# Re-ordered start and end of an attention block: four queries and half of the modulation ahead of the first scores, low parts ahead of the last reciprocals

## The reference

```python
mod = (silu(c) @ wmod).reshape(16, 6, 1, 256)      # sa, ca, ga, sb, cb, gb
ga, gb = sign(ga) * max(|ga|, 0.25), sign(gb) * max(|gb|, 0.25)
h = layernorm(x) * (1 + ca) + sa
q, kv = h @ Wq.T, h @ Wkv_down.T                   # 8 heads of 64; latent of 64
x = x + ga * (softmax(q @ (kv @ Wk_up.T).T / 8) @ (kv @ Wv_up.T)) @ Wo.T
h = layernorm(x) * (1 + cb) + sb
x = x + gb * (h @ weight.T + pooled(h) @ disha)    # pooled: sums of h over 4 pieces of 64
```

## Time and profile before

| | us |
|---|---|
| median of 3 runs | 3176.31 (3176.28 to 3179.29) |
| the profiled execution, its own time | 3175.94 |
| its span, first to last instruction | 3174.1 |
| PE busy in the span | 3115.8 (98%) |
| POOL busy | 2556.5 (81%) |
| DVE busy | 2295.4 (72%) |
| ACT busy | 1729.6 (54%) |

### The profile page before, as it was taken

How to read it: one execution, slowest core, us unless ns; L and a number is a source line. 1 busy time by engine, 2 the same in 40 slices (tenths; PEclk the granted TensorE clock), 3 DMA queues, 4 the chain that set the end, 5 groups by cost and what they waited for, 6 DMA issues and landing times.

```text
span 3174.1 us, 44918 instructions
## 1 busy us (share of the span) xinstructions
PE 3115.8 (98%) x15394; PEld 1907.2 (60%) x15394; DVE 2295.4 (72%) x2466; ACT 1729.6 (54%) x3209; POOL 2556.5 (81%) x1521
## 2 busy tenths in 40 slices
PE   6999999999999999999999999999999999999997
PEld 5556656556665665656566565666656656565555
DVE  5667777776777777777777777767777777776764
ACT  3555555555555555555555555555555555555543
POOL 2888787888878888787887878888788887887886
PEclk8999999999999999999999999999999999999998
DMA  2111111111111111111111111111111111111111
GB/s 83 41 44 58 49 53 44 52 60 44 55 54 58 48 41 58 48 64 48 44 61 44 57 45 48 64 44 54 51 61 46 43 57 48 61 44 38 55 44 40
DMA packets 161250, 162.89 MB, mean 51 GB/s; under 512 B 58112, under 2 KB 109440, under 8 KB 161024
## 3 DMA queue, kind: packets, MB, share of 16 engines
q1 hardware_dynamic: 161024, 160.03, 15.4%
HBM read 74.40 MB, written 17.33 MB: 29 GB/s over the span
## 4 chain that ended last, share of the span: by engine, by line
PE 88%; DVE 4%; issue 3%; ACT 2%; POOL 2%; DMA 1%; SPq 0%; POOLq 0%; ACTq 0%; DVEq 0%
PE ps_mix L601 26%; PE ps_score L622 15%; PE ps_max L647 14%; PE ps_score L624 13%; PE ps_side L587 7%; PE ps_side L713 4%; PE ps_side L732 3%; PE ps_side L699 2%; POOL prob_sum L987 2%; DVE neg_max L1138 1%; ACT probs L818 1%; PE ps_side L720 1%; PE ps_side L689 1%; PE ps_side L665 1%; DVE mixed L1106 1%
## 5 line engine op out<-in xcount | busy, mean ns | idle before, releaser
L987 POOL TENSOR_TENSOR prob_sum<-prob_sum,probs 128x1024 f32<-128x1024 f32 x768 | 1890.5, 2462 | 317.1 <-ACT probs L818 242.8
L1138 DVE TENSOR_REDUCE neg_max<-ps_max 128x1 f32<-128x1024 f32 x1024 | 1238.0, 1218 | 420.6 <-PE ps_max L647 411.5
L818 ACT ACTIVATE probs<-ps_score 128x512 f32<-128x512 f32 x2048 | 1112.5, 596 | 548.5 <-PE ps_score L624 537.7
L601 PE MATMUL ps_mix<-probs,values 128*64 128x512 f32 x4096 | 935.4, 598 | 0.8 <-ACT probs L818 0.8
L622 PE MATMUL ps_score<-query,key_hi 128*128 128x512 f32 x2048 | 877.3, 428 | 9.3 <-DVE query L1176 6.1
L624 PE MATMUL ps_score<-query_m,key_lo 128*128 128x512 f32 x2048 | 806.1, 394 | 0.0
L647 PE MATMUL ps_max<-key_hi,query 128*128 128x512 f32 x2048 | 642.6, 395 | 11.9 <-DVE neg_max L1138 11.5
L601 PEld LDWEIGHTS ps_mix<-probs,values 128*64 128x64 f32 x4096 | 271.3, 136 | 531.0 <-issue 529.8
L622 PEld LDWEIGHTS ps_score<-query,key_hi 128*128 128x128 f32 x2048 | 384.1, 188 | 255.1 <-ACT probs L818 102.3
L647 PEld LDWEIGHTS ps_max<-key_hi,query 128*128 128x128 f32 x2048 | 380.9, 188 | 112.2 <-DVE neg_max L1138 20.8
L987 POOL TENSOR_TENSOR prob_sum<-probs 128x1024 f32<-128x1024 f32 x128 | 319.3, 2495 | 129.2 <-ACT probs L818 129.2
(11 more groups left out here) (200 smaller groups left out, 2833.8 us busy)
## 6 DMA issues: line engine op xcount, KB each, us to landing
query_m<-query SPq DMA_DIRECT2D x128, 512.0 KB, 3.2
recip<-recip_scratch SPq DMA_DIRECT2D x254, 128.0 KB, 2.9
x_in<-in_L_attn_x_dram SPq DMA_DIRECT2D x32, 512.0 KB, 4.6
x_mid<-in_L_attn_x_dram SPq DMA_DIRECT2D x64, 256.0 KB, 3.7
out_dram<-x_mid SPq DMA_DIRECT2D x64, 256.0 KB, 2.2
denoms<-recip SPq DMA_DIRECT2D x508, 1.0 KB, 1.7
gates<-gates_scratch SPq DMA_DIRECT2D x16, 256.0 KB, 4.3
query_m<-max_row SPq DMA_DIRECT2D x128, 4.0 KB
```

The source lines that it names most:

```text
L601: last = nc.tensor.matmul(ps_mix[j * R:j * R + R, :], values[par][:, k, :], probs[:, (STEPS * z.c + s) % RING, j * HALF:(j + 1) * HALF], s ...
L818: nc.scalar.activation(probs[:, (STEPS * z.c + s) % RING, half * HALF:(half + 1) * HALF], ps_score[half], ACT.Exp, scale=SCALE).then_inc(e ...
L987: nc.gpsimd.tensor_tensor(out=total[:, :], in0=before, in1=probs[:, now % RING, :], op=ALU.add).then_inc(adds_done, 1)
L1138: nc.vector.tensor_reduce(neg_max[:, m:m + 1], ps_max[m % 2][:, :], AX_X, ALU.max, negate=True).then_inc(maxima_done, 1)
```

## The change

Nothing of the arithmetic changes except the number of instructions in three places.

1. **Head.** PE makes only half of the modulation (16 of 32 matmuls) ahead of the first projections; the other half becomes a side piece `mod_out` on step 57. DVE writes batch 0's `mod1` itself, and POOL's copy of it is gone from the head.
2. **Head.** Only queries 0 to 3 are made in slot -1 (before: 0 to 5). Queries 4 to 7 move to steps 0, 2, 4 and 6 of slot 0 (before: 6 and 7, on steps 0 and 4). Query 0 goes ahead of the second `latent`. Two of four `wo_fold` pieces move to steps 10 and 14 of slot 0, both `weight_t` to steps 18 and 22.
3. **Head.** Statistics and `apply` for the first half of batch 1 move from step 63 of slot -1 into slot 0 (statistics on step 1, apply on step 2); those of the second half from steps 1 and 2 to steps 3 and 4.
4. **Tail.** `mixed_hi` and `mixed_lo` of chunks 0 and 1 go ahead of `divide_last` in ACT's and DVE's queues, `mixed_lo` of chunk 2 right behind it, and `out_proj` of all four chunks onto four consecutive steps ahead of the first `norm2_t`. In `divide_last` each reciprocal is followed by its multiplication. `FFN_HI` of the tail goes from step 3 to 2.
5. **Everywhere.** `w_ffn_lo` becomes two instructions of 256 columns: on steps 21 and 23 of a middle slot, both on step 2 of the tail.

```diff
-FFN_GATE, FFN_HI, FFN_LO = (1, 19), (3, 21), (3, 21)
+FFN_GATE, FFN_HI, FFN_LO = (1, 19), (2, 21), ((2, 2), (21, 23))
...
 LAST = {
-    "mixed_hi": (1, 2, 5, 6),
-    "mixed_lo": (1, 2, 5, 6),
-    "out_proj": (2, 4, 8, 10),
-    "norm2": (4, 5, 9, 11),
-    "norm2_t": (7, 9, 12, 13),
-    "h2_split": (7, 9, 12, 13),
-    "ffn": (9, 11, 14, 15),
+    "mixed_hi": (0, 0, 2, 2),
+    "mixed_lo": (0, 0, 1, 2),
+    "out_proj": (1, 2, 3, 4),
+    "norm2": (3, 4, 5, 6),
+    "norm2_t": (5, 6, 8, 10),
+    "h2_split": (5, 6, 8, 10),
+    "ffn": (7, 9, 11, 12),
 }
...
-    "query": (10, 12, 53, 57, 62, 63) + PLAN["query"][6:],
-    "wo_t": (49, 51),
-    "gate": (52,),
-    "wo_fold": (53, 55, 56, 59),
-    "values_t": (54, 60),
-    "weight_t": (61, 62),
+    "query": (7, 58, 62, 63, STEPS, STEPS + 2, STEPS + 4, STEPS + 6),
+    "values_t": (11, 12),
+    "wo_t": (54, 56),
+    "gate": (56,),
+    "mod_out": (57,),
+    "wo_fold": (60, STEPS + 10, 60, STEPS + 14),
+    "weight_t": (STEPS + 18, STEPS + 22),
...
-            for j, part in enumerate((1, 0, 4, 3)):
...
+            modulate(ps_max[0], (1, 0)).then_inc(mod_made, 1)
...
                             if i == 0:
-                                need(act, mod1_set, b + 1)
+                                need(act, mod1_set, b)
+                                act.wait_ge(mod1_made, 2)
...
-                    if s == NEXT_APPLY and z.has_n:
-
-                        if first(z):
-                            apply(0, 0)
+                    if s == NEXT_APPLY and z.n in (0, 1):
+                        apply(z.n, 0)
+                    if s == (NEXT_APPLY + 2 if z.n == 1 else NEXT_APPLY) and z.has_n:
                         apply(z.n, 1)
...
+            for j, add in ((0, 1.0), (1, 0.0)):
+                nc.vector.tensor_scalar(mod1[:, 2 * j:2 * j + 2].rearrange("p (b j) -> p b j", b=1), cols[:, 0:1, 2 * j:2 * j + 2], add, None,
+                                        ALU.add).then_inc(mod1_made, 1)
...
-                        need(dve, group_evacuated, GROUPS * (b + 1))
-                        for q in range(CT):
-                            raw = mixed_block(1 - z.par, PAIRS - 1, 1)[:, q * QC:(q + 1) * QC]
                             if q < CT - 1:
+                                need(dve, group_evacuated, GROUPS * (b + 1))
                                 need_alone(dve, recips_done, GROUPS * b + i + 1 + q)
...
-                    if s == FFN_LO[z.has_c] and z.has_o:
-                        need(dve, w_ffn_hi_done, z.o + 1)
-                        nc.vector.tensor_tensor(w_ffn_lo[:, :, :], w_ffn_gated, w_ffn_hi[:, :, :].bitcast(F32),
-                                                ALU.subtract).then_inc(w_ffn_split, 1)
+                    for k in range(NF):
+                        if s == FFN_LO[z.has_c][k] and z.has_o:
+                            need(dve, w_ffn_hi_done, z.o + 1)
+                            nc.vector.tensor_tensor(w_ffn_lo[:, k, :], w_ffn_gated[:, k, :], w_ffn_hi[:, k, :].bitcast(F32),
+                                                    ALU.subtract).then_inc(w_ffn_split, 1)
...
-                        if z.has_nn and s == (STEPS - 1 if first(z) else t):
+                        if z.has_nn and not first(z) and s == t:
                             statistics(z.n + 1, 0, i)
```

More of the change, by code:

```diff
@@ L152, in _pieces @@
         found = []
-        for rank, (kind, (count, which)) in enumerate([*PIECES.items(), *(FOLDS.items() if self.c < 0 else ())]):
+        kinds = [*PIECES.items(), *(FOLDS.items() if self.c <= 0 else ())]
+        if self.c == 0:
+            for rank, (kind, (count, which)) in enumerate(kinds):
+                for i in range(count):
+                    if kind in FIRST and FIRST[kind][i] >= STEPS:
+                        found.append((FIRST[kind][i] - STEPS, rank, kind, i, 0))
+        for rank, (kind, (count, which)) in enumerate(kinds):
             for i in range(count):
+                if self.c == 0 and (kind in FOLDS or kind in FIRST and self.step(kind, i) >= STEPS):
+                    continue
                 s = self.step(kind, i)
@@ L170, in rooms, with place @@
         return FIRST_ROOMS if self.c < 0 else (0,) if self.has_c else LAST_ROOMS
-    def place(self, kind, i):
-        at = [(k, j) for (_, _, k, j, _) in self.pieces].index((kind, i))
+    def place(self, kind, i, which=None):
+        at = [k == kind and j == i and which in (None, w) for (_, _, k, j, w) in self.pieces].index(True)
         rooms = self.rooms()
@@ L327, in adaln_block, with full, drained, query_drained @@
             ps_max[i][:, h * HALF:(h + 1) * HALF] for i in range(2) for h in range(2)]
-        def full(eng, z, kind, i, wait=need):
-            room, count = z.place(kind, i)
+        def full(eng, z, kind, i, wait=need, which=None):
+            room, count = z.place(kind, i, which)
             wait(eng, side_full[room], count + 1)
-        def drained(eng, z, kind, i, wait=need):
-            room, count = z.place(kind, i)
+        def drained(eng, z, kind, i, wait=need, which=None):
+            room, count = z.place(kind, i, which)
             wait(eng, side_drained[room], count + 1)
+        def query_drained(eng, b, i, wait=need):
+            late = PLAN["query"][i] >= STEPS or b == 0 and FIRST["query"][i] >= STEPS
+            drained(eng, flagged(b if late else b - 1), "query", i, wait, 0 if late else 1)
         def last_full(eng, z):
@@ L557, in _, with modulate @@
         def _(pe):
+            def modulate(bank, parts):
+                for j, part in enumerate(parts):
+                    for f in range(NF):
+                        for k in range(NF):
+                            last = nc.tensor.matmul(bank[:, (2 * j + f) * B:(2 * j + f + 1) * B],
+                                                    s_wmod[:, k, part * D + f * P:part * D + (f + 1) * P],
+                                                    s_silu[:, 2, k, :], start=(k == 0), stop=(k == NF - 1))
+                return last
             pe.wait_ge(consts_made, 3)
@@ L573, in _ @@
             pe.wait_ge(silu_steps, 3)
-            for j, part in enumerate((1, 0, 4, 3)):
[L575 to L578, removed]
-                                                s_silu[:, 2, k, :], start=(k == 0), stop=(k == NF - 1))
-            last.then_inc(mod_made, 1)
+            modulate(ps_max[0], (1, 0)).then_inc(mod_made, 1)
             pe.wait_ge(fold_a_kept, 6)
@@ L655, in side_work @@
                 for kind, i, b, w in z.at(s):
-                    room, count = z.place(kind, i)
+                    room, count = z.place(kind, i, w)
                     side = rooms[room]
@@ L743, in side_work @@
                                                         s_wmod[:, k, part * D:(part + 1) * D], start=(k == 0), stop=(k == NF - 1))
+                    elif kind == "mod_out":
+                        pe.wait_ge(side_drained[room], count)
+                        last = modulate(side, (4, 3))
                     elif kind == "wo_fold":
@@ L1183, in slot @@
                                                     key_hi[1 - z.par][:, cols].bitcast(F32), ALU.subtract).then_inc(side_drained[room], 1)
+                        elif kind == "mod_out":
+                            dve.wait_ge(side_full[room], count + 1)
+                            cols = side[:, 0:4 * B].rearrange("p (j b) -> p b j", b=B)
+                            nc.vector.tensor_scalar(mod_cols[:, :, 4:6], cols[:, :, 0:2], 1.0, None, ALU.add)
+                            nc.vector.tensor_scalar(mod_cols[:, :, 6:8], cols[:, :, 2:4], 0.0, None,
+                                                    ALU.add).then_inc(side_drained[room], 1)
                         elif kind == "weight_t":
```

41 lines of the change are left out of this document (21 added, 20 removed).

## The result

The changed kernel takes **3158.41 us** (median of 4 runs, 3158.12 to 3160.31). The kernel before, run beside it on the same chip, took 3177.8 (3176.28 to 3180.22); the ratio is 0.9937, 95% interval 0.9924 to 0.9950. The forecast was 3158.7.

The account below looks back on a forecast made before the run. PE was taken to be full from step 9 of slot 0, with engine-hopping chains bounding head and tail. Terms -1.3, -5.0 and -11.3 sum to -17.6 from 3175.94, giving 3158.3, put at 3158.7 us for the median; range 3150 to 3169.

Parts of the forecast that it names:

- The sum: Whole kernel: head with slot 0 -1.3, middle slots -5.0, tail -11.3, together -17.6 us.
- Head up to the first maxima: Head: first maxima start at 36.8 instead of 41.1 us, from gains of 1.3 and 3.0 us.
- Maxima to scores: Head, first maxima to first scores: 30.3 us becomes 26.9, so first scores start at 63.7, 7.7 us earlier.
- The 0.9 of extra wait at `mod_out`: Head, step 57: DVE runs dry while PE does the moved modulation half of 3.5 us, adding 0.9 us of wait.
- Slot 0: Slot 0 pays back: first denominator 3.9 us later relative to first scores (34.4), plus 2.5 us of PE work.
- The 2.5 us of added PE work: Slot 0, behind the first denominator: two `wo_fold` pieces of 1.00 us and two `weight_t` of 0.25 added to full PE.
- Middle: Middle slots: the shorter first piece of `w_ffn_lo` saves 0.33 us in each of 15 slots, 5.0; bounds 0 and 7.5.
- The rival that nothing moves: Middle slots: the low part ends where a POOL add ends, whatever its length; 3163.7 us, chance 0.20.
- the whole wait: Middle slots, upper bound of the gain: all of PE's 0.5 us wait goes in 15 slots, 7.5 us.
- that rival: Middle slots: the piece on step 23 sits out an add of 2.38 us and PE waits; +23, 3199 us, chance 0.04.
- Tail: Tail: early `out_proj` gains 5.9 us, then POOL's four `norm2` chunks of 2.65 bound it; -11.3 us, bounds -14 and -6.
- The held add: Tail: `mixed_lo` 0 gets the port first and holds back POOL's last add by 1.1 us; bounds 0.3 and 2.4.

## Why the prediction was right

**The sum.** Forecast -1.3, -5.0 and -11.3. Between the two profiles it was -2.6, -2.5 and -12.4; by the single parts timed, -1.3, -5.1 and -11.4. The total, 17.6, was met by both countings (17.5 and 17.8; the timed whole is -20.0, interval -24.2 to -15.9), but the head and middle terms aren't as sure as that: both are smaller than the 4.0 us by which profiles with the same head differ (slot 1's copy at 250.8 to 254.8). That the time came within 0.3 us of the forecast is partly luck: the kernel before ran 1.5 us above the time from which the sum started, and the timed gain was 20.0, not 17.6.

**Head up to the first maxima.** Forecast 36.8, measured 36.84 (36.84 to 38.40 in three traces). `w_in_lo` holds POOL off for 1.2 (charged: 1.4), transposes at 23.60 (normed x forecast at 23.7). That the second latent runs at the full clock was right here, but now the first doesn't: which matmuls are slow changes from profile to profile, 6 to 13 of them in the old head. The Trainium skill, "TensorE: Matmul & The Clock Gate", Part 1, says that the number of slow matmuls at the start varies from run to run of the same kernel; the table above agrees.

**Maxima to scores.** Forecast 26.9 us, measured 25.8 (24.5 to 25.9). The 0.9 of extra wait at `mod_out` didn't come: the piece took 1.85 us and not 3.5, and DVE stood idle for 0.47 at it. **Slot 0.** First sum 34.4 after the first scores forecast, 34.1 measured (30.1 to 30.6 before). The 2.5 us of added PE work: from the first sum to slot 1's copy it was 152.6 us before and is 155.2 now, 2.6. Averaged over six and three traces, slot 1's copy moved from 253.7 to 252.3: -1.3.

**Middle.** The mechanism was right, the size of its term wrong twice. The first half saved 0.25 of its 2.09 us and not 0.33, as 256 columns take 0.41 alone and not half of 0.66, and it still sat out most of an add. And the sum has fifteen slots where fourteen have the wait: with four of PE's 18 waits in the head and early slot 0, as the prediction says, 14 are left. A slot became 0.24 shorter in the changed kernel and 0.27 with the halves alone, 3.4 and 3.8 in fourteen, against 5.0. The rival that nothing moves (3163.7) is refuted by the rows, and the second half didn't stall PE: it takes 0.41 in slot 1, where that rival had a whole add ahead of it. The greater miss is the bound: the text let "the whole wait" be 0.5 us a slot, and it was 0.9 to 1.0.

**Tail.** The held add: +0.75 by its row, charged 1.1. Only the first low part went ahead of it, as charged; the second sat it out (3.36 us in place of 1.22), ended within 0.1 of the ones-matmuls, as forecast, and cost nothing more. `out_proj` 0 and 1 at full clock: yes. POOL's `norm2` starts at 3135.84, on the old clock (5.1 later) 3140.9, against 3142.7 forecast. Its four chunks take 12.5 us, not 10.6: 1.9 more, where 0.7 was charged for port conflicts. The first instruction, which the profile starts while `mixed_lo` 3 is on DVE, takes 1.05 in place of 0.24, and two more in the third chunk, beside DVE's `h_lo`, are longer by 0.9 together. The last add ends at 3159.1 on the old clock, forecast 3160.1. The early start and the longer chunks largely cancel. What the prediction had wrong in kind was where the gain lies: it gave 5.9 us to the first two chunks and the rest to the steps behind; alone the first two give 2.8.

## What to carry to other kernels

Before halving an instruction that PE waits behind, look for a step where it can stand whole: the number of its step was worth 16.5 us, cutting it in two 5.1. When a short PE stall recurs, price it by start-to-start times beside an undisturbed copy of the same sequence, not by the idle time shown. In a tail, data made ready earlier are worth little until the in-order engine's queue is rearranged so that nothing ready stands behind something that isn't; test the two halves together.

## What the runs showed of the hardware that was not expected

- A short PE stall in this stream of matmuls costs 0.4 to 0.5 us more than the idle time shown: 0.26 shown cost 0.66 in the rows and 0.73 by the slots; 0.50 shown cost 0.88 in the rows and 0.99 by the slots.
- The level of TensorE's clock in the first latents differs between profiles of the same head (0 to 10 slow matmuls in the new, 6 to 13 in the old). In the old head it moves the first maxima by up to 1.9 us relative to the modulation, 0.19 us for each slow matmul from the second latent on.
- The modulation starts when its weights have landed, 16.55 to 18.73 us after the start in these traces, whatever the kernel. Together with the clock this is why single profiles can't show a head's gain of one or two us.
